# The first sweep of a fused SwiGLU+LoRA kernel: block B12 kept in the tiles of T3 and T2, the first gate/up weights loaded earlier, the last features' LoRA product moved behind P2

## The reference

```python
x = x + causal_conv(x * mask, K) + D * x * mask, masked      # S4-style kernel K per token row, length 1024
gate = x @ W_gate.T + 0.5 * B_gate[idx] @ (A_gate[idx] @ x)  # 2752 features; adapter idx per sequence, rank 16
up   = x @ W_up.T   + 0.5 * B_up[idx]   @ (A_up[idx] @ x)
act  = silu(gate) * up
x = x + act @ W_down.T + 0.5 * B_down[idx] @ (A_down[idx] @ act)
```

## Time and profile before

| what | value |
|---|---|
| median of 3 runs | 1727.62 us (1727.45 to 1730.32) |
| the profiled execution, its own time | 1727.99 us |
| span in its profile | 1726.3 us, mean granted PE clock 0.984 |
| busy, share of the span | PE 94%, DVE 53%, ACT 33%, POOL 7% |
| chain that ended last | PE 87%, DMA 6%, DVE 4%, issue 2%, ACT 1% |
| 200 to 300 us | PE busy 81.73 of 100, granted clock 0.91 |
| 300 to 600 us | PE busy 100%, clock 1.00 |

### The profile page before, as it was taken

One profiled execution on the slowest core, in us unless ns is written; L12 is line 12 of the kernel. 1 busy time (PEld: TensorE's weight loads), 2 busy tenths in 40 slices (PEclk: granted clock), 3 DMA queues, 4 the chain that ended last, 5 costly groups with the idle time before them and its releaser, 6 DMA issues.

```text
span 1726.3 us, 21064 instructions
## 1 busy us (share of the span) xinstructions
PE 1631.1 (94%) x8224; PEld 1396.0 (81%) x8224; DVE 920.6 (53%) x1182; ACT 566.5 (33%) x678; POOL 114.1 (7%) x185
## 2 busy tenths in 40 slices
PE   2989969999999998799999999998999999999999
PEld 2988858888888886678888888886888888888887
DVE  6544576666655664876655666655325325324422
ACT  2211253333333333443333333334215215224311
POOL 5000003432220000000000000000000000000000
PEclk9999989999999999899999999999999999999999
DMA  8989526675553335323333333327447557547652
GB/s 311 359 322 333 207 85 194 195 210 163 168 167 120 98 98 164 111 87 100 101 98 98 98 98 99 98 73 243 149 134 243 158 142 225 169 137 220 175 141 60
DMA packets 156869, 278.40 MB, mean 161 GB/s; under 512 B 55554, under 2 KB 72770, under 8 KB 156226
## 3 DMA queue, kind: packets, MB, share of 16 engines
q1 hardware_dynamic: 104034, 234.19, 42.6%
q0 software_dynamic: 12672, 25.82, 4.8%
q10 hardware_dynamic: 40064, 17.04, 3.5%
HBM read 237.26 MB, written 65.31 MB: 175 GB/s over the span
## 4 chain that ended last, share of the span: by engine, by line
PE 87%; DMA 6%; DVE 4%; issue 2%; ACT 1%; SPq 0%; DVEq 0%; ACTq 0%
PE ps L783 81%; PE ps L768 6%; DMA tt<-k_pad 2%; DMA k_pad<-ksb 1%; DMA raw<-a_gu_sel 1%; DVE xlo L1499 1%; DMA xraw<-x_keep 1%; DMA x_keep<-xt 1%; DVE wlo L1499 1%; ACT whi L977 0%; DVE xraw L1499 0%; DMA draw<-act_keep 0%; ACT b12hi L977 0%; DVE xres L1693 0%; DMA leni<-len 0%
## 5 line engine op out<-in xcount | busy, mean ns | idle before, releaser
L783 PE MATMUL ps<-xhi,whi 128*128 128x512 f32 (+1 forms) x1080 | 420.1, 389 | 25.8 <-DVE gq L1621 10.0
L783 PE MATMUL ps<-xlo,whi 128*128 128x512 f32 (+1 forms) x1080 | 419.3, 388 | 0.0
L783 PE MATMUL ps<-xhi,wlo 128*128 128x512 f32 (+1 forms) x1080 | 418.2, 387 | 0.0
L977 ACT ACTIVATE whi<-raw 128x1024 fp32r<-128x1024 f32 (+3 forms) x202 | 198.0, 981 | 577.5 <-PE ps L783 542.8
L1499 DVE TENSOR_TENSOR wlo<-raw,whi 128x1024 fp32r<-128x1024 f32 (+1 forms) x190 | 219.3, 1155 | 307.0 <-ACT whi L977 306.7
L783 PE MATMUL ps<-dhi,whi 128*128 128x512 f32 (+2 forms) x760 | 288.0, 379 | 3.7 <-DVE xres L1693 3.7
L783 PE MATMUL ps<-dlo,whi 128*128 128x512 f32 (+2 forms) x760 | 286.7, 377 | 0.0
L783 PE MATMUL ps<-dhi,wlo 128*128 128x512 f32 (+2 forms) x760 | 286.4, 377 | 0.0
L783 PEld LDWEIGHTS ps<-xhi,whi 128*128 128x128 f32 x1080 | 206.2, 191 | 65.4 <-DVE gq L1621 10.7
L783 PEld LDWEIGHTS ps<-xhi,wlo 128*128 128x128 f32 x1080 | 205.5, 190 | 41.3
L783 PEld LDWEIGHTS ps<-xlo,whi 128*128 128x128 f32 x1080 | 206.1, 191 | 37.4
(11 more groups left out here) (168 smaller groups left out, 1670.8 us busy)
## 6 DMA issues: line engine op xcount, KB each, us to landing
raw<-wgu SPq DMA_DIRECT2D x84, 512.0 KB, 6.6
tt<-k_pad SPq DMA_DIRECT2D x64, 512.0 KB, 8.0
raw<-wd SPq DMA_DIRECT2D x64, 512.0 KB, 3.8
loraw<-bgu_sel SPq DMA_DIRECT2D x84, 256.0 KB, 4.4
act_keep<-up SPq DMA_DIRECT2D x42, 512.0 KB, 3.1
draw<-act_keep SPq DMA_DIRECT2D x84, 256.0 KB, 7.0
raw<-wd SPq DMA_DIRECT2D x32, 320.0 KB, 3.0
xr<-xr SPq DMA_DIRECT2D x4, 2048.0 KB, 10.5
```

Source lines behind the costliest of these rows:

```text
L783: return nc.tensor.matmul(out, w, x, start=start, stop=stop, skip_group_check=True)
L977: return nc.scalar.activation(out, in_, ACT.Copy)
```

## The change

1. B12's halves of the first sweep go to `c12hi` and `c12lo`, which lie in the tiles of xhi that T2 and T3 use later. B12's hi no longer waits for the store of `xt`; the hi of T3 and of T2 wait for `pro(0, 6)`, the end of `rest_main(0, "B")`, instead. `sums_13(0)` waits for nothing on PE.
2. SP issues the last `x1_store` ahead of agB1's load, loads up 0 once agB0 is split and gate 0 once agB1 is split, each ahead of `bl`.
3. On PE `rest_lora` A and B move from the prologue to behind P2 of the sweep's first tile, in both sweeps. The signals are counted in a table (`SIGNAL`): `rest_main` B is now 6, `rest_lora` A and B are 7 and 8, behind P2.
4. ACT and DVE get a new order in the first sweep.

```diff
+        c12hi = place("c12hi", X0 + 5 * QB, [2 * KB], F32R)
+        c12lo = place("c12lo", X0 + 4 * QB, [2 * KB], F32R)
...
             load_ag(0, "B", 0)
+            x1_store(HQ - 1)
             wait_lo("wl", 0)
             load_ag(0, "B", 1)
-            x1_store(HQ - 1)
+            wait_lo("agB0", 0)
+            load_raw(("up", 0), wgu_d[0, :, KB:2 * KB])
+            wait_lo("agB1", 0)
+            load_raw(("gate", 0), wgu_d[0, :, 0:KB])
             sp.wait_ge(s_x1st, 16 * HQ)
             sp.wait_ge(s_xform, xform(0, "T4"))
             sp.wait_ge(s_xhi, xsplit(0, "B12"))
             load_bl(0)
-            wait_lo("agB0", 0)
-            wait_lo("agB1", 0)
-            load_pair(0)
...
                 for p in PRODUCTS:
                     product(p)
+                    if f == 0 and p == "P2":
+                        for x in "AB":
+                            rest_lora(u, x)
...
                     lora_a(u, "B")
-                    rest_lora(u, "A")
                     rest_main(u, "B")
-                    rest_lora(u, "B")
...
-                    if q == "B12":
-                        act.wait_ge(s_x1st, 16 * HQ)
...
+                    if u == 0 and q in ("T3", "T2"):
+                        act.wait_ge(s_p, pro(0, 6))
...
             x_hi(0, "T1", "post")
             t_hi(0, "A")
+            w_hi("u0", 0)
+            w_hi("bl", 0)
+            t_hi(0, "B")
             x_hi(0, "T3")
-            w_hi("u0", 0)
+            w_hi("u1", 0)
             x_hi(0, "T2")
-            w_hi("bl", 0)
+            w_hi("u2", 0)
             x_hi(0, "T4")
-            t_hi(0, "B")
-            w_hi("u1", 0)
             rest_parts(0, "A")
-            w_hi("u2", 0)
             rest_parts(0, "B")
...
-                if n % FT == 0:
-                    dve.wait_ge(s_p, pro(n // FT, 7))
+                if n == FT:
+                    dve.wait_ge(s_p, pro(1, 6))
...
             x_lo(0, "B22")
+            x_lo(0, "B12")
             x_form(0, "T1", "post")
+            w_lo("agB0", 0)
+            w_lo("agB1", 0)
             x_form(0, "T3")
-            x_lo(0, "B12")
             x_form(0, "T2")
             x_form(0, "T4")
-            w_lo("agB0", 0)
-            w_lo("agB1", 0)
+            x_lo(0, "T1", "post")
             t_mask(0, "A")
-            x_lo(0, "T1", "post")
             t_lo(0, "A")
-            x_lo(0, "T3")
             w_lo("u0", 0)
             t_mask(0, "B")
-            x_lo(0, "T2")
             w_lo("bl", 0)
-            x_lo(0, "T4")
             t_lo(0, "B")
             sums_13(0)
+            x_lo(0, "T3")
             w_lo("u1", 0)
+            sums_24(0)
+            x_lo(0, "T2")
+            w_lo("u2", 0)
+            x_lo(0, "T4")
             rest_act(0, "A")
-            sums_24(0)
-            w_lo("u2", 0)
             rest_act(0, "B")
```

More of the change, by code:

```diff
@@ L50, with order_of_signals @@
 PRO = 8
+def order_of_signals():
+    at = {}
+    for u in range(NU):
+        keys = [("pro", u, i) for i in range(1, 7)]
+        for n in range(FT * u, FT * (u + 1)):
+            for p in PRODUCTS:
+                keys.append(("prod", n, p))
+                if n == FT * u and p == "P2":
+                    keys += [("pro", u, 7), ("pro", u, 8)]
+        for k in keys:
+            at[k] = len(at) + 1
+    return at
+SIGNAL = order_of_signals()
 def pro(u, i):
-    return u * (PRO + 7 * FT) + i
+    return SIGNAL["pro", u, i]
 def prod(n, p):
-    return PRO * (n // FT + 1) + 7 * n + PRODUCTS.index(p) + 1
+    return SIGNAL["prod", n, p]
 END_GU = prod(N - 1, "P3")
@@ L402, in x_source, with x_split, x_tile @@
             return v[:, :, 0:HQ - 1] if part == "pre" else v[:, :, HQ - 1:HQ]
-        def x_split(q, hi):
+        def x_split(u, q, hi):
             if q == "B12":
-                return (b12hi if hi else b12lo)[:, :]
+                return ((b12hi if hi else b12lo) if u else (c12hi if hi else c12lo))[:, :]
             return (xhi if hi else xlo)[:, QUAD[q], :]
-        def x_tile(q, hi, c, g=None):
-            v = quad_view(x_split(q, hi))
+        def x_tile(u, q, hi, c, g=None):
+            v = quad_view(x_split(u, q, hi))
             return v[:, :, c, :] if g is None else v[:, HQ * g:HQ * (g + 1), c, :]
@@ L432, in slot_free @@
                 if i % FT == 0:
-                    return pro(i // FT, {"u0": 4, "u1": 5, "u2": 7}[kind])
+                    return pro(i // FT, {"u0": 4, "u1": 5, "u2": 6}[kind])
                 return prod(i - 1, {"u0": "P2", "u1": "P7", "u2": "P4"}[kind])
@@ L809, in lora_a @@
                         q = block_col(x, k)
-                        last = passes(half(ps[4 + i], g), tile(whi, g, k), tile(wlo, g, k), x_tile(q, True, k % 4, g),
-                                      x_tile(q, False, k % 4, g), k == 0 and g == 0, k == C - 1)
+                        last = passes(half(ps[4 + i], g), tile(whi, g, k), tile(wlo, g, k), x_tile(u, q, True, k % 4, g),
+                                      x_tile(u, q, False, k % 4, g), k == 0 and g == 0, k == C - 1)
                     done(last)
@@ L820, in rest_main @@
                     q = block_col(x, k)
-                    last = passes(ps[6 + i], tile(whi, 2, k), tile(wlo, 2, k), x_tile(q, True, k % 4),
-                                  x_tile(q, False, k % 4), k == 0)
+                    last = passes(ps[6 + i], tile(whi, 2, k), tile(wlo, 2, k), x_tile(u, q, True, k % 4),
+                                  x_tile(u, q, False, k % 4), k == 0)
                 done(last)
@@ L871, in product @@
                         at = slice((k0 + k) * P, (k0 + k + 1) * P)
-                        last = passes(out, w[0][:, at], w[1][:, at], x_tile(q, True, k), x_tile(q, False, k),
+                        last = passes(out, w[0][:, at], w[1][:, at], x_tile(u, q, True, k), x_tile(u, q, False, k),
                                       k == 0 and p in ("P1", "P2", "P5", "P7"))
@@ L1050, in x_hi @@
                         act.wait_ge(s_p, prod(FT - 1, "P1" if q == "B11" else "P2"))
-                copy(part_of(x_split(q, True), part), x_source(u, q, part)).then_inc(s_xhi, 1)
+                copy(part_of(x_split(u, q, True), part), x_source(u, q, part)).then_inc(s_xhi, 1)
             def t_hi(u, x):
@@ L1578, in x_lo @@
                     dve.wait_ge(s_cev, HH * (HQ - 1) if part == "pre" else H)
-                sub(part_of(x_split(q, False), part), x_source(u, q, part),
-                    part_of(x_split(q, True), part).bitcast(F32)).then_inc(s_xlo, 1)
+                sub(part_of(x_split(u, q, False), part), x_source(u, q, part),
+                    part_of(x_split(u, q, True), part).bitcast(F32)).then_inc(s_xlo, 1)
             def by_batch(x):
```

## The result

The changed kernel takes 1717.88 us (median of 10 runs, 1715.87 to 1725.52) against 1728.05 us for the kernel before (10 runs, 1726.79 to 1730.32). The ratio is 0.9943, 95% interval 0.9934 to 0.9951: 8.5 to 11.4 us faster. The forecast of 1716.6 us from 1727.62 is a ratio of 0.9936, inside that interval. One execution in the study, of the experiment that puts rest_lora back in both sweeps, took 2446.29 us at a mean granted clock of 0.632; that experiment's ratio leaves it out.

What follows compares the result with a forecast made beforehand. PE bounds the kernel, busy nearly everywhere, with holes of 10.20, 4.72 and 0.78 us up to P6. P6 earlier 11.4, clock -1.3, second sweep 0.9 sum to 11.0 us: 1716.6 us from 1727.62, range 1712.5 to 1721.

Steps and rivals of the forecast that it cites:

- The prologue without holes: On PE, lora_a B starts when rest_main A ends; P1 starts at 227.45, 1 us after rest_main B.
- When agB1 lands: agB1's load in the prologue lands at 212.5, between 209.4 and 215.8; its low starts at 213.65.
- The tail: Late ACT and DVE work in the first sweep's start: P7's LoRA product waits 4.4 us and ends near 246.
- P6: First sweep: P6 starts at 248.6 instead of 259.99, 11.4 us earlier, with 3.8 us for the second rest store.
- The clock: PE falls to half clock behind the new holes, at P6; 1.3 us lost, from 0 to 2.6.
- The second sweep: At its start P1 and P2 run in PE's 3.27 us hole; 0.9 us come off, bounds 0 and 1.5.
- The sum: Whole kernel: 11.4 - 1.3 + 0.9 = 11.0 us off.
- The yardstick: P6's start in the first sweep: each microsecond earlier is one off the end.
- agB1 wasn't late: Rival one: agB1 lands at 215.8 in the prologue, everything 3.3 us later, 1720 to 1721.5 us; chance 0.16.
- the second sweep's start shifted as a block: Rival four said no: transfers there come at their own times, giving back the front's gain, 1727 us; chance 0.04.
- rival three: Slower: load_pair(1), sharing engines with the gathers, lands late and delays P6; landing at 264 gives 1732 us; chance 0.03.

Runs made afterwards that it cites:

- the wait at d: Changed kernel with the wait for the two rest stores moved from c1 (ACT) to d (DVE), both sweeps: 1715.24 us, ratio 0.9913.
- The late store: Changed kernel with the last store of xt issued behind agB1's load, as before the change: 1718.5 us, ratio 0.9938.
- the new tail: Changed kernel with ACT and DVE reordered at the end of the first sweep's start, rest parts ahead of u2: 1712.7 us, ratio 0.9903.

## Why the prediction was right

- *The prologue without holes*: right. lora_a B follows rest_main A. rest_main B ended later than I had it, since lora_a A itself ran partly at half clock in this profile; P1 began near +24.0, worked out from P5 at 233.58 less two rest_lora (1.4) and two products (5.5); my time was +23.5, behind a hole of 1 us, and u0's low had ended at 225.11, so the hole I expected there and the one before P5 didn't open. Where lora_a A ran at full clock (the wait at d) P1 began at +22.5 and the hole before P5 was 0.80 us, for 1 us forecast.
- *When agB1 lands*: the time was near, the mechanism incomplete. I had its low at +9.7 from the landing of the load; it was at +8.6. The load landed at 209.94, or +7.2 for my +8.6, and the slot in whi became free at about the same time. The late store shows the slot to be the bound: 1.7 us less for the load changed nothing. I hadn't priced the slot at all. It cost little: even with part of lora_a A at half clock the slot came free only 0.2 to 0.3 us behind the load. This put P7's LoRA 0.9 us sooner than forecast (+40.6 for +41.5).
- *The tail*: right. T4, the rest parts, u3 and lora on DVE follow at the steps read from rows 4 and 5. The holes were forecast at 4.4 and 2.5 us and were 4.09 and 1.88. Behind the table load (236.78, 1.28 us) silu started at 238.07, with no drain between.
- *P6*: +43.7 and +44.9 in two profiles, forecast +44.7 (248.6). The store took 3.8 and 4.9 us; I had 3.8.
- *The clock*: right in kind, undersized in the first profile. I took 1.3 us with 2.6 as the bound; P6 to P3 took 9.05 - 6.48 = 2.6 us longer there, and 8.40 - 6.48 = 1.9 in the second. P6's being early by a microsecond and the clock's loss being greater cancel, which is luck: P3 came 9.8 and 9.3 us sooner, and 11.4 - 1.3 = 10.1 was forecast.
- *The second sweep*: 0.8 us from lora_a B to P3 in both profiles of the changed kernel, forecast 0.9; undoing that part cost 1.9 and 0.6 in one profile each.
- *The sum*: 10.9 us from +0 to the end for 11.0 forecast is closer than the parts are. The first sweep's start gave 9.8 and 9.3 us and the second's 0.8; PE's wait at the end of the first sweep, which the prediction doesn't touch, was 0.4 and 1.1 us shorter than in the one profile of the kernel before, and made up the difference.
- *The yardstick*: a microsecond at P6 was not one off the end. P6 moved by 1.2 us between two profiles of the changed kernel whose stretches from +0 to the end differ by 0.1. In the second less of the half clock fell on P6 (8.40 us to P3 instead of 9.05), so that P3 moved by 0.5 only, and PE's wait at the end of the sweep was 0.7 shorter.
- *The rivals*: agB1 wasn't late; gate 1's load, issued among the gathers, never held c1 up (u0(1)'s hi at 241.89 follows the instruction before it); the second sweep's start shifted as a block, by 10.2 us. One sum is off in rival three: a landing at 264 puts P6 at 266.1, 17.5 us behind the forecast's, which is 1734 and not 1732; its chance doesn't hang on that.

The runs also say what the change is made of. I had treated B12's new place as what frees the front. Shown is something else: the place and the early store are each nearly enough (3.3 and 0 us lost when one is undone, 9.2 when both are), and little of it is left unless rest_lora leaves the prologue (8.0 of the 10.9 us lost). The early weights are worth 1.8 us at P7's LoRA. The new order on ACT and DVE was never undone by itself, so its share is open.

## What to carry to other kernels

Two edits that each take away the same wait are substitutes: undo them one at a time and both look cheap; only undoing both shows what the wait is worth. Where a wait guards a buffer, put it at the first instruction that overwrites it, not at the head of the stage; here c1 waited for both rest stores and doesn't touch their buffer, and moving that wait to d took the hole before P6 away. When a stage is short of one engine's work, order that engine by when the others need each result, and count a hole on PE at its length plus what the half clock behind it costs.

## What the runs showed of the hardware that was not expected

- Short holes can cost the clock too. Behind 1.64 and 2.08 us of idling PE was granted 0.50 between 246 and 249 us (the new tail), but behind 1.64 and 0.41 it stayed at 1.00, in one profile each. In the changed kernel's profile lora_a A ran in part at 0.50 behind a hole of 2.57 us, as the stretch below shows. The same hole was followed by half clock in ten of the twelve profiles, and lora_a A took 7.3 us; in the profile of the kernel before and in that with the wait at d the clock stayed full, and it took 5.8. So the length of the hole alone doesn't tell.

```profile
204.00:205.00 1.00, 1.00 (x7) 1.00 (x6) 0.42 (x2) 1.00 (x2) 0.00 (x0) 0.52 1.04 391
205.00:206.00 1.00, 1.00 (x6) 1.00 (x6) 1.00 (x1) 1.00 (x1) 0.00 (x0) 0.50 1.03 383
```

- A store of 128 KB among the gathers took 3.8 and 4.9 us in two profiles of the same code and 5.2 us with the late store; over the eleven profiles of the changed kernel and its variants it took 3.5 to 5.2.
- A load of 512 KB issued 3.4 us behind a store of 2 MB on the same queue landed after 5.9 us, and the store after 8.0; with the load ahead they took 4.2 and 9.5. By the Trainium skill (DMA: Bandwidth & Descriptors, Queues, rings and completion order) descriptors are consumed in ring order on each DMA engine, which doesn't fix the order in which transfers complete. What was seen agrees: the load landed 1.3 us behind the store (209.94 and 208.65), and with the load ahead it landed first.
- The first matmul of lora_a A started anywhere within 4.8 us between profiles, though nothing differs ahead of it; profiles of this kernel are comparable only from a fixed point behind the convolution.
